# One core, selective scan and routed experts: ScalarE's steps spread over the units, one combination per bank of y and block, products with C dealt 2, 2, 1, 0 a quad, routing comparison by columns, other head and tail

## What is computed

```
xn    = layernorm(x)                                  # over channels
x_dbl = xn @ x_proj_w.T                               # 128 + 16 (B) + 16 (C)
delta = softplus(x_dbl[:128] @ dt_proj_w.T + dt_proj_b)
state = exp(delta * A) * state + delta * B * xn       # scan over the 512 tokens, 16 states a channel
y     = sum_n(state * C) + xn * D
logits = xn @ gate_w + gate_b                         # 8 experts, the best 2 of each token
f     = mean over the 2 of relu(xn @ expert_w[e] + expert_b[e])
out   = x + y * silu(f)
```

## Time and profile before

| | |
|---|---|
| runs | 2283.3, 2288.0, 2279.07 us, median 2283.3 |
| profiled execution | 2277.99 us |
| its span, first to last instruction | 2276.2 us |
| granted PE clock, mean | 0.93 |
| busy share of the span | DVE 87%, POOL 83%, PE 81%, ACT 61% |
| DMA | 641.47 MB, 282 GB/s in the mean |

### The profile page before, as it was taken

One profiled execution on the slowest core, in us unless ns is written; L12 is line 12 of the kernel. 1 busy time (PEld: TensorE's weight loads), 2 busy tenths in 40 slices (PEclk: granted clock), 3 DMA queues, 4 the chain that ended last, 5 costly groups with the idle time before them and its releaser, 6 DMA issues.

```text
span 2276.2 us, 35000 instructions
## 1 busy us (share of the span) xinstructions
PE 1843.6 (81%) x8688; PEld 1192.7 (52%) x8688; DVE 1983.9 (87%) x3002; ACT 1378.6 (61%) x2370; POOL 1888.0 (83%) x1146
## 2 busy tenths in 40 slices
PE   2597988979788797888969888797987979888883
PEld 2364655546455564555546555465654646565552
DVE  3688898999889998899988989899888999989985
ACT  2465666666476665666656576565665666566663
POOL 2679889888888988889888988789888898898993
PEclk8698999989899998998989999899998999999997
DMA  5868798788968878798887978789797897987974
GB/s 212 291 229 336 238 345 279 266 323 256 365 199 308 310 259 327 232 327 290 262 309 240 367 245 295 278 258 367 222 323 258 267 352 228 360 269 265 337 253 127
DMA packets 281729, 641.47 MB, mean 282 GB/s; under 512 B 22529, under 2 KB 23041, under 8 KB 273297
## 3 DMA queue, kind: packets, MB, share of 16 engines
q1 hardware_dynamic: 187792, 445.84, 55.2%
q10 hardware_dynamic: 69120, 125.86, 15.6%
q0 software_dynamic: 24576, 67.13, 10.6%
HBM read 516.58 MB, written 122.16 MB: 281 GB/s over the span
## 4 chain that ended last, share of the span: by engine, by line
DVE 28%; PE 24%; issue 23%; POOL 12%; ACT 9%; ACTq 2%; DVEq 1%; DMA 1%; POOLq 0%; SPq 0%
PE z_ps L1028 12%; DVE scan_ps L881 7%; POOL dbx L444 6%; DVE p_sb L891 6%; DVE h_sb L881 4%; POOL xs_rows L470 4%; ACT scan_ps L597 3%; PE y_ps L1045 3%; PE proj_ps L980 2%; PE y_ps L1062 1%; POOL pp_sb L458 1%; DVE proj_ps L786 1%; PE proj_ps L972 1%; DVE stats L747 1%; PE xt_ps L1015 1%
## 5 line engine op out<-in xcount | busy, mean ns | idle before, releaser
L444 POOL TENSOR_TENSOR dbx<-b_sb,u_sb 128x1024 f32<-128x1024 f32 x512 | 1226.0, 2467 | 109.0 <-issue 41.1
L597 ACT ACTIVATE scan_ps<-delta,a_sb 128x512 f32<-128x512 f32 x1024 | 697.3, 688 | 645.2 <-DVE p_sb L891 612.2
L1028 PE MATMUL z_ps<-w_sb,xsT 128*128 128x512 f32 x1920 | 912.5, 620 | 111.1 <-ACT r_sb L618 111.0
L881 DVE TENSOR_TENSOR_SCAN scan_ps<-scan_ps,dbx 128x512 f32<-128x512 f32 x704 | 842.4, 1217 | 164.3 <-ACT scan_ps L597 138.6
L1028 PEld LDWEIGHTS z_ps<-w_sb,xsT 128*128 128x128 f32 x1920 | 360.8, 198 | 501.9 <-issue 501.5
L1045 PE MATMUL y_ps<-ident,p_sb 128*128 128x128 f32 x2816 | 430.3, 286 | 190.2 <-DVE p_sb L891 189.2
L458 POOL TENSOR_TENSOR pp_sb<-h_sb,c_sb 128x512 f32<-128x512 f32 (+1 forms) x256 | 404.9, 1582 | 163.1 <-PE y_ps L1062 143.8
L1045 PEld LDWEIGHTS y_ps<-ident,p_sb 128*128 128x128 f32 x2816 | 341.6, 146 | 354.4 <-DVE p_sb L891 238.3
L891 DVE TENSOR_TENSOR p_sb<-scan_ps,c_sb 128x512 f32<-128x512 f32 x704 | 473.4, 673 | 0.0
L881 DVE TENSOR_TENSOR_SCAN h_sb<-scan_ps,dbx 128x512 f32<-128x512 f32 x320 | 387.3, 1210 | 3.3 <-ACT scan_ps L597 3.2
L1030 PE MATMUL z_ps<-eb_sb,expert_hot 128*128 128x512 f32 x240 | 190.9, 796 | 0.0
(11 more groups left out here) (99 smaller groups left out, 1405.2 us busy)
## 6 DMA issues: line engine op xcount, KB each, us to landing
w_sb<-in_ew SPq DMA_DIRECT2D x240, 1024.0 KB
b_sb<-bc_rows SPq DMA_DIRECT2D x64, 1024.0 KB, 10.9
xs<-xs_rows ACTq DMA_DIRECT2D x240, 256.0 KB
ys_rows<-r_sb ACTq DMA_DIRECT2D x240, 256.0 KB
c_sb<-bc_rows SPq DMA_DIRECT2D x64, 768.0 KB, 14.7
xn<-in_x SPq DMA_DIRECT2D x16, 1024.0 KB, 15.7
c_sb<-bc_rows SPq DMA_DIRECT2D x64, 256.0 KB, 15.9
xo<-in_x SPq DMA_DIRECT2D x64, 256.0 KB
```

The lines of the kernel that those rows point to most:

```text
L444: nc.gpsimd.tensor_tensor(dbx[:, k % DBX_PAIRS], b_sb[:, 2 * m:2 * m + 2, :], u_sb[:, dt % 2, :].unsqueeze(1).to_broadcast([P, 2, T]), ALU ...
L597: nc.scalar.activation(scan_ps[:, j % DA_BANKS, :], delta[:, dt % 2, :], ACT.Exp, scale=a_sb[:, dt, n:n + 1]).then_inc(da_ready, 1)
L881: nc.vector.tensor_tensor_scan(state, bank, dbx[:, j // 2 % DBX_PAIRS, r % 2, :], 0.0, ALU.mult, ALU.add).then_inc(scanned, 1)
L1028: nc.tensor.matmul(z_ps[:], xsT[:, slot, c, :], w_sb[:, i % WRING, c, :], start=(c == 0), stop=False)
```

## The change

- **POOL_C.** From (1, 2, 1, 1, 1, 1, 1, 2, 2, 2, 1, 1, 1, 1, 1, 1) to 2, 2, 1, 0 in each block. That is 20 of 64 units on POOL both times, in 12 instructions in place of 16. The last quad of a block has none, so the last product of a batch (unit 63) is DVE's; it is issued behind the first scan of the next batch.
- **Banks.** The ring of three banks takes the same bank for units 59 and 60 and then goes round a batch without a break; before, units 63 and 0 shared one.
- **ACT.** Copies of y at units 24, 40, 56 and 9 in place of 28, 44, 60 and 12; the parts of the sigmoids and the copies spread out; row loads and stores first in a unit; the product with D of block 0 at unit 62 of the batch before.
- **Combinations.** One in each block (units 29, 45, 59, and 12 of the batch after), each in the bank of y that was just copied, in place of two and two in blocks 1 and 2.
- **Softplus.** `DVE_LAG` 8 in place of 6; the steps `Z1` and `NZ0` one unit earlier and two later.
- **Routing.** `hot` is written by eight comparisons of nine columns with one number a partition, in place of two over 32 elements with both inputs broadcast. `rank` comes at unit 39 (38), the scatter behind quads 11, 12 and 13 with 3, 3 and 2 parts (10, 11, 12 with 2, 3, 3).
- **SP.** The loads of B and C for the next batch are interleaved otherwise with those of the weights.
- **Head.** In batch 0 the layer norm of batch 1 starts at unit 11 (2); `gate(0)` comes ahead of `delta_u(0, 0, 0)`; PE no longer waits for `eb_step` at its start; SP loads the first two row tiles, before it loads x of batch 1 (ACT did, at units 5 and 6).
- **Tail.** In the last batch tile i comes at unit 5 + 3.4 i (the last at 52, not 58), the combinations of batch 14 all fall in it, and the four of batch 15 use four different PSUM banks.

Core of the diff:

```diff
-POOL_C = (1, 2, 1, 1, 1, 1, 1, 2, 2, 2, 1, 1, 1, 1, 1, 1)
+POOL_C = (2, 2, 1, 0)
+LAST_TILE_AT = {5 + (i * 34) // 10: i for i in range(TILES)}
-DVE_LAG = 6
+DVE_LAG = 8
+FRONT = {"stats": (2, 3, 4, 5), "var": 5, "root": 8, "apply": (11, 13, 14, 15), "gate": 32, "rank": 39}
+FIRST_FRONT = {"stats": (11, 11, 12, 12), "var": 13, "root": 16, "apply": (19, 19, 20, 20), "gate": 37, "rank": 44}
+FIRST_STEPS = {1: "Z1", 9: "Z2", 21: "NT0", 23: "NT1", 25: "NT2", 27: "NT3", 29: "NX0", 31: "NX1", 33: "Z3",
+               40: "NK", 45: "NR", 46: "NS", 50: "NZ0"}
-SIG_AT = (28, 32, 44, 48)
-OUT_AT = (29, 32, 45, 48)
+COPY_Y_AT = {24: 0, 40: 1, 56: 2, 9: 3}
+SIG_AT = ((26, 28, 29), (43, 44, 45), (57, 58, 59), (10, 11, 12))
-SCATTER_AT = {10: (0, 1), 11: (2, 3, 4), 12: (5, 6, 7)}
+SCATTER_AT = {11: (0, 1, 2), 12: (3, 4, 5), 13: (6, 7)}
...
+        def bank_of(j):
+            return (j if j <= AGAIN else j - 1) % DA_BANKS
...
+        def z_buf(b, tt):
+            if is_last(b):
+                return (proj_ps[:], xt_ps[:].rearrange("p c q -> p (c q)"), z_ps[:],
+                        y_ps[:, 0].rearrange("p t q -> p (t q)"))[tt]
+            if not z_in_y(b, tt):
+                return proj_ps[:]
+            return y_ps[:, tt % 2].rearrange("p t q -> p (t q)")
...
             zero_rows(0)
             send_bc(0)
...
             load_w(0, 0)
+            load_first_rows(0)
+            load_first_rows(1)
             load_x(1)
...
                 act.wait_ge(out_sum, from_start(b * TT + tt))
                 nc.scalar.activation(z, acc[:, tt], ACT.Exp, scale=-1.0).then_inc(sig_step, 1)
...
-                nc.vector.tensor_tensor(hot[:, :, 0:TT], iota[:, 0:E].unsqueeze(2).to_broadcast([P, E, TT]),
-                                        topf[:, :, 0].unsqueeze(1).to_broadcast([P, E, TT]),
-                                        ALU.is_equal)
-                nc.vector.tensor_tensor(hot[:, :, TT:BLK], iota[:, 0:E].unsqueeze(2).to_broadcast([P, E, TT]),
-                                        topf[:, :, 1].unsqueeze(1).to_broadcast([P, E, TT]),
-                                        ALU.is_equal).then_inc(hot_ready, 1)
+                for k in range(2):
+                    for tt in range(TT):
+                        last = nc.vector.tensor_scalar(hot[:, :, k * TT + tt], iota[:, 0:E + 1], topf[:, tt, k:k + 1], None,
+                                                       ALU.is_equal)
+                last.then_inc(hot_ready, 1)
...
+                    if j == 0 and not is_first(b):
+                        times_c(b - 1, UNITS - 1)
...
             pe.wait_ge(const_p, CONST_P)
-            pe.wait_ge(eb_step, 7)
```

More of the change, by code:

```diff
@@ L72, in build @@
     CONST_P = CONST + E + 4
-    ND = [QUAD - c for c in POOL_C]
+    ND = [QUAD - POOL_C[q % NQ] for q in range(QUADS)]
     DVE_C = sum(ND)
+    POOL_QUADS = [q for q in range(QUADS) if POOL_C[q % NQ]]
+    PQ = len(POOL_QUADS) // DT
     ctx = ExitStack()
@@ L141, in build @@
         topf = sb("topf", [P, TT, 2])
[L142 removed]
+        hot = sb("hot", [P, E + 1, BLK])
         place = sb("place", [P, E, BLK])
@@ L238, in next_step, with steps_at, front_at, tiles_at @@
             return step_no(None, name) if is_first(b) else step_no(b - 1, name)
+        def steps_at(b):
+            return FIRST_STEPS if is_first(b) else STEPS
+        def front_at(b):
+            return FIRST_FRONT if is_first(b) else FRONT
+        def tiles_at(b):
+            return LAST_TILE_AT if is_last(b) else TILE_AT
+        def sig_at(b):
+            return LAST_SIG_AT if is_last(b) else SIG_AT
         def delta_step(b, dt):
             return next_step(b, "NZ0") if dt == 0 else step_no(b, f"Z{dt}")
-        def back(j, ring):
-            return ring if j >= ring else j + UNITS - max(i for i in range(UNITS) if i % ring == j)
+        def bank_of(j):
+            return (j if j <= AGAIN else j - 1) % DA_BANKS
+        def back(j):
+            return next(i for i in range(1, UNITS) if bank_of((j - i) % UNITS) == bank_of(j))
         def on_dve(j):
@@ L690, in batch @@
                     for part in range(3):
-                        name = STEPS.get(j - COPY_LAG - part)
+                        name = steps.get(j - COPY_LAG - part)
                         if name == "NZ0" and nxt:
@@ L740, in _ @@
                 for part in range(3):
-                    sigmoid(B - 1, tt, B * DT, part)
+                    sigmoid(B - 1, tt, part)
         @block.vector
@@ L1059, in add_y_quad @@
                 pe.wait_ge(pp_ready, quad_no(b, q) + 1)
-                for i in range(POOL_C[q]):
+                for i in range(QUAD - ND[q]):
                     for tt in range(TT):
-                        last = nc.tensor.matmul(y[:, tt, :], pp_sb[:, q % 2, i, tt * P:(tt + 1) * P], ident[:],
-                                                start=False, stop=(q % NQ == NQ - 1 and i == POOL_C[q] - 1),
+                        last = nc.tensor.matmul(y[:, tt, :],
+                                                pp_sb[:, POOL_QUADS.index(q) % 2, i, tt * P:(tt + 1) * P], ident[:],
+                                                start=False, stop=(q % NQ == PQ - 1 and i == QUAD - ND[q] - 1),
                                                 is_transpose=True, skip_group_check=True)
@@ L1088, in batch @@
             def batch(b, par, pair):
+                steps, tiles = steps_at(b), tiles_at(b)
                 for j in range(UNITS):
-                    name = STEPS.get(j)
+                    name = steps.get(j)
                     if name and name[0] == "N":
```

281 lines of the change are left out of this document (150 added, 131 removed).

## The result

The change takes 2314.56 us in the median of its runs (2310.97 to 2317.76); the kernel before, with one more run beside them, 2281.19. The ratio is 1.0143, 95% interval 1.0112 to 1.0175. It is slower by 1.4%, where 2202 was forecast and "faster" held a chance of 0.83. The time lies outside the range.

A forecast was written before the change was run, and what follows sets the result against it. DVE was the busiest engine, POOL next, so the prediction asked what DVE idles for. Head -18.7, tail -8 and -3.6 a batch (-54 over 15) sum to -80.7 us: 2202 against the median, range 2130 to 2268.

The forecast's parts named there:

- `rank`, +3.7 (0 to +4.6): DVE's ranking now runs while POOL computes: first instruction held about 1.5 us, second 2.3; +3.7 us a batch.
- rival 2: `rank` isn't held because POOL stands then, so no +3.7: 2146 us; chance 0.22.
- Routing comparison, -1.3: Eight column comparisons at the routing, never held, take 1.05 us a batch in place of 2.45: -1.3; other end +16.4.
- Rival 1: Each of the eight routing columns waits for a POOL instruction to end: +17.7 us a batch, 2468 us; chance 0.10.
- Copy at 56, -2.7: DVE's waits of 4.15 and 1.24 us at this copy of y go: mean -2.7 us a batch, ends 0 and -2.7.
- Copy at 24, -1.9: Of 4.4 us of DVE waits at this copy of y, 2.5 stay: -1.9 us a batch, ends 0 and -4.4.
- rival 3: Stalls only move: copy waits return at the relu or projection's copy, -1.9 and -2.7 lost: 2271 us; chance 0.18.
- POOL, -0.9: Four fewer POOL instructions and no standing for `row_u`: DVE's 1.17 us wait for POOL mostly goes, -0.9 a batch.
- Head, -18.7: Batch 0: unit 10's product comes 22.6 us earlier, less 3.9 of layer norm to come: -18.7, from -12 to -21.
- Tail, -8: At the end, POOL's first gather starts 6.3 us ahead of DVE's end, not 2.9 behind: -8, ends -3 and -9.2.
- I am wrong if those pairs stay above 272: Sign: two successive batches take about 267 us in place of 274.5; above 272, waits elsewhere, refutes the forecast.
- The likeliest forecast: The main case, all terms as summed with `rank` held: 2202 us; chance 0.42.

The follow-up runs named there:

- experiment 5: The change with rank's expert numbers in PSUM and row numbers written by the sum itself, without the CAST, second gather at quad 8: 2228.53 us, ratio 0.9768.
- experiment 14: The change with PE's delta projection for the next batch (NZ0) at unit 47 and nothing else: 2289.56 us, ratio 1.0052.
- experiment 8: The kernel of experiment 6 with PE's delta projection (NZ0) at unit 47 in place of 48: 2191.86 us, ratio 0.9608.
- experiment 3: The kernel before with rank one unit later (39) and the scatter a quad later: 2365.19 us, ratio 1.0391.
- experiment 7: The kernel of experiment 6 with block 0's copy of y at unit 26 in place of 24, its sigmoid at 27, 29, 30: 2244.01 us, ratio 0.9846.
- experiment 4: The change with the last part of the second gather at quad 7 in place of 8: 2275.83 us, ratio 0.9991.
- experiment 6: The kernel of experiment 5 with the last part of the second gather at quad 7 in place of 8: 2219.96 us, ratio 0.9722.
- experiment 1: The change with rank's expert numbers in a PSUM bank, the CAST of row numbers kept: 2313.69 us, ratio 1.0164.
- experiment 10: The kernel of experiment 8 with the copy of y at unit 26 and the old routing comparison, two over 32 elements: 2191.11 us, ratio 0.9605.

## Why the prediction was wrong

Two steps failed. The term for `rank` had the right mechanism but little more than half its size, and the new order brought waits for PE that the sum put at nothing.

- **`rank`, +3.7 (0 to +4.6).** It had the mechanism, and took one POOL instruction as the longest a hold can last. Measured: +6.85 in 14 batches, 96 us where the sum had 56. With nothing to hold, 85 us come back (experiment 5). Its upper end was the length of two POOL instructions, from a head in which they don't overlap.
- **New waits for PE, put at nothing.** Without any hold (experiment 5) the ratio is 0.9768, or 2228 us against the median of the kernel before; for a `rank` that isn't held the prediction gave 2146 (rival 2). So 82 us of the miss lie elsewhere. NZ0 stood in the list of changes and not in the sum: 1.9 us a batch in the rows, 21 us in the change (experiment 14), 26 without the hold (experiment 8). The two waits at unit 34 are 2.5 a batch, 37 us in 15 batches by the rows; no run removes them alone.
- **Routing comparison, -1.3.** Right in the change (1.17 for 2.45), by luck: "they were never held" rested on L763 and L860. L860 is held once POOL computes at its place (2.4 us in experiment 3), and its successor takes 2.38 in the head of the change. L763, one column, never is. By themselves, in the kernel before, the columns cost +5.3 a batch. Rival 1 had the right mechanism; its condition, that POOL computes at the gate, failed because POOL stood 8.45 us for PE. It priced all eight as held, and three are.
- **Copy at 56, -2.7.** Right: the waits of 4.15 and 1.24 are gone, though NZ0's 1.88 stands in the same quarter, which gained 2.0.
- **Copy at 24, -1.9.** 3.27, 0.84 and 0.29 became 2.78 and 0.65, which is -1.0. With the 2.5 at unit 34 the stretch has more idle time than before, not less. That the waits come back further on is what rival 3 said, and moving the copy once more moves them again (experiment 7). That the copy's move in the change caused those at unit 34 isn't shown.
- **POOL, -0.9.** The wait of 1.17 for POOL's pair is gone from the rows, as forecast.
- **Head, -18.7.** The scan of unit 16 comes 18.5 earlier, but by a different sum: the 2 to 5 us of waiting for x near unit 11 aren't there, and 6.95 for ACT are. The term was added to the end without asking whether batch 0 keeps it. The trace keeps 10.9 a batch later, and undoing the head's units (not its other parts) costs at most 8 in the medians and nothing between the profiled executions.
- **Tail, -8.** The last three quarters of batch 15 and what follows are 10.1 shorter (+43.1 at unit 16, +33.0 at the end). Behind DVE's last product it is 5.8 of them, since POOL's last product waited for PE.
- **The sum.** The time is 112 us above the forecast. `rank` makes 40 of them, unit 34 some 37, NZ0 21 to 28, the copy at 24 some 13, and the head 8. That is a little more than the miss, so some 10 us were gained where no term stands; which ones is open.
- **The bet.** "I am wrong if those pairs stay above 272": they are 283.5. The likeliest forecast and rival 2 asked whether `rank` is held; neither asked for how long. Rival 3 asked where waits go, and priced them as coming back in full, not as growing.

Still open: why POOL's instructions overlap behind a gather, what keeps DVE out then, and what the waits at unit 34 cost by themselves. That they overlap, and for how long DVE is held, the traces of the change and of experiment 4 show.

## What to carry to other kernels

An instruction of VectorE that reads and writes SBUF alone can wait for GpSimd however small it is. Here a TENSOR_SCALAR over 9 or 15 columns, a CAST over 8 or 15 and a TENSOR_TENSOR over 32 did; a TENSOR_SCALAR over one column and a TENSOR_REDUCE did not. What it costs is set by what GpSimd does at that moment. It was up to one GpSimd instruction of 2.37 us where these don't overlap, and all of the work ahead, 7 us, where they do. Before such an instruction is moved by a unit, or split into many, read GpSimd's rows at that time. Better, give it an operand in PSUM or fold it into a reduction: in experiments 5 and 6 it no longer mattered where GpSimd's work stood. And a gain measured in time at one unit is worth only what the next bottleneck leaves of it: follow it to the end of the batch.

## What the runs showed that was not expected

- A DVE instruction over 15 elements took 7.0 us in 14 of 16 batches, behind three POOL instructions, and 0.18 with its operands in PSUM (experiments 1 and 5), though POOL computed in 15 of 16 batches.
- TENSOR_REDUCE from SBUF to SBUF, next to the held ones, was never held: 0.25 to 0.28 us in all 16 batches, also when it wrote whole numbers (experiment 5).
- POOL's 128x1024 products are recorded 2.9 us long at a step of 2.3 behind a gather, and 2.37 at the same step otherwise.
- The old comparison, two inputs broadcast, can be held through several POOL instructions too: 5.74 us in experiment 10.
- Moving `rank` by one unit and the scatter by a quad costs the kernel before 3.9%.
